# Gather, pair products and quad-diagonal moments of a recommendation tower: loops unrolled, weights laid out by the host, masks by VectorE, steps of eight groups, four row buffers

## The reference

```python
e = stack([tbl_f[ids[:, f]] for f in range(26)], axis=1)      # 512 x 26 x 32
def _cin_layer(x_prev, x0, W, b):
    return einsum('bik,bjk,hij->bhk', x_prev, x0, W) + b[None, :, None]
x1 = _cin_layer(e, e, W1, b1)                                  # W1: 128 x 26 x 26
x2 = _cin_layer(x1, e, W2, b2)                                 # W2: 128 x 128 x 26
z = sum(concatenate([x1, x2], axis=1), axis=-1)                # 512 x 256
h = concatenate([z, dense_ctx], axis=1)                        # 512 x 272
h = maximum(h @ W_top1 + b_top1, 0.0)                          # 512 columns
h = maximum(h @ W_top2 + b_top2, 0.0)                          # 256 columns
y = h @ W_top3                                                 # 512 x 1
```

## Time and profile before

| | |
|---|---|
| Median of three timed runs | 189.18 us (188.01 to 190.05) |
| Span of the profiled execution, first to last instruction | 269.0 us |
| The profiled execution's own time, with what lies around the span | not recorded for this run |
| PE / DVE / ACT / POOL busy | 171.1 / 94.1 / 103.7 / 109.4 us |
| Mean granted PE clock in the span | 0.797 of full speed |
| Instructions | 3544 |

### The profile page before, as it was taken

How to read it: one execution, slowest core, us unless ns; L and a number is a source line. 1 busy time by engine, 2 the same in 40 slices (tenths; PEclk the granted TensorE clock), 3 DMA queues, 4 the chain that set the end, 5 groups by cost and what they waited for, 6 DMA issues and landing times.

```text
span 269.0 us, 3544 instructions
## 1 busy us (share of the span) xinstructions
PE 171.1 (64%) x1239; PEld 158.7 (59%) x1239; DVE 94.1 (35%) x370; ACT 103.7 (39%) x267; POOL 109.4 (41%) x110
## 2 busy tenths in 40 slices
PE   7900594209929388986300799954001999899997
PEld 7800583209729287976300789954002999888985
DVE  0576003210943086920000568500003569047200
ACT  1020330019595165494000462951003463966313
POOL 3778777720077400577774003877770000000000
PEclk9975598556997869996555599995555799999999
DMA  6700011000001000011000000001000000000000
GB/s 240 250 12 13 12 14 14 13 7 0 0 10 17 11 1 4 2 12 15 14 12 10 0 0 2 11 12 15 12 12 2 0 0 0 0 0 0 0 0 3
DMA packets 5729, 5.08 MB, mean 19 GB/s; under 512 B 2875, under 2 KB 5061, under 8 KB 5718
## 3 DMA queue, kind: packets, MB, share of 16 engines
q0 software_dynamic: 3328, 1.71, 4.7%
q1 hardware_dynamic: 1698, 2.34, 2.6%
q10 hardware_dynamic: 692, 0.89, 1.0%
HBM read 4.93 MB, written 0.00 MB: 18 GB/s over the span
## 4 chain that ended last, share of the span: by engine, by line
PE 35%; another core or an unknown queue 30%; ACT 15%; DVE 9%; issue 9%; POOL 0%; DVEq 0%; ACTq 0%; POOLq 0%
PE bank L321 9%; ACT diag L467 8%; PE bank L287 4%; DVE t L650 4%; PE bank L322 4%; PE bank L281 4%; PE bank L256 3%; PE bank L332 2%; DVE prod L771 2%; PE bank L372 1%; ACT w2t L432 1%; ACT t L486 1%; DVE prod L616 1%; PE bank L275 1%
## 5 line engine op out<-in xcount | busy, mean ns | idle before, releaser
L242 POOL DMA_INDIRECT rows<-in_tbl_dram,idx x104 | 108.7, 1045 | 91.1 <-DVE prod L616 57.4
L321 PE MATMUL bank<-diag,prod 128*128 128x108 f32 x256 | 60.7, 336 | 56.0 <-DVE t L650 44.3
L321 PEld LDWEIGHTS bank<-diag,prod 128*128 128x128 f32 x256 | 46.6, 227 | 59.5 <-issue 59.5
L650 DVE COPY t<-bank 13x64 f32<-13x64 f32 (+2 forms) x128 | 26.7, 209 | 108.6 <-ACT t L487 66.7
L322 PE MATMUL bank<-diag,prod 128*77 128x64 f32 x256 | 41.7, 249 | 0.3 <-issue 0.3
L322 PEld LDWEIGHTS bank<-diag,prod 128*77 128x77 f32 x256 | 36.8, 173 | 0.5 <-issue 0.5
L485 ACT COPY t<-bank 55x128 f32<-55x128 f32 x32 | 8.3, 259 | 71.9 <-remote 47.8
L467 ACT COPY diag<-prod 32x416 f32<-32x416 f32 (+2 forms) x48 | 33.4, 696 | 1.0
L287 PE MATMUL bank<-w1ab,w2t 128*128 128x169 f32 x52 | 16.0, 489 | 14.6 <-ACT folded L434 9.7
L287 PEld LDWEIGHTS bank<-w1ab,w2t 128*128 128x128 f32 x52 | 12.8, 278 | 17.5 <-ACT folded L434 10.4
L281 PE MATMUL bank<-w1s,w2t 128*128 128x183 f32 x52 | 10.8, 377 | 16.4 <-ACT w2t L432 15.6
(11 more groups left out here) (79 smaller groups left out, 186.3 us busy)
## 6 DMA issues: line engine op xcount, KB each, us to landing
rows<-in_tbl_dram,idx POOLq DMA_INDIRECT x104
wt<-in_W_top_dram SPq DMA_DIRECT2D x2, 512.0 KB
w<-in_L_rec_W_dram ACTq DMA_DIRECT2D x1, 832.0 KB
w<-in_L_rec_W_dram SPq DMA_DIRECT2D x1, 832.0 KB
w<-in_L_rec_W_dram SPq DMA_DIRECT2D x1, 338.0 KB
idx<-in_ids_dram SPq DMA_DIRECT2D x4, 13.0 KB
vec<-in_L_rec_b_dram ACTq DMA_DIRECT2D x2, 0.5 KB
dctx<-in_dense_ctx_dram ACTq DMA_DIRECT2D x1, 32.0 KB
```

The lines of the kernel that those rows point to most:

```text
L242: pool.indirect_dma_start(rows[:, f, :], None, tables[f], bass.IndirectOffsetOnAxis(ap=idx[i][:, f:f + 1], axis=0)).then_inc(s_got[part], 16)
L321: nc.tensor.matmul(m0[:, g * P:g * P + JW * QUADS], prod[:, G, 0:P], mov, start=True, stop=True)
L650: ins = nc.vector.tensor_copy(t1[p0:p0 + HALF, GRAM + slot:GRAM + slot + nb, n].rearrange("p j (g r) -> p j g r", r=QUADS), m1[64:64 + HAL ...
```

## The change

What is added, moved and removed, engine by engine:

- Host: `layouts` hands over W2 already transposed, the two halves of the symmetrized W1 in the column order of the pairs (`w1p`) and in transposed form (`w1t`), the vectors as columns, the dense context transposed and the indices of all tiles side by side. PE's transposes of W2, W1, vectors and context and ACT's copies of them go, as do DVE's 30 small operations that symmetrized W1. One DVE addition over 521 columns takes their place, and one for `z1w` (five blocks of 128 columns).
- Gathers: four row buffers and all indices from the start. POOL waits for nothing but the indices; its loop is unrolled.
- Masks: ACT's twelve copies in a tile (`fill_diag`) go. DVE writes `diag` with one multiplication for each part (`fields_in`), of the fields (repeated four times) by a 0/1 mask `quad`. That is a DVE operation with two inputs in SBUF of 13, 10 and 3 fields x 4 columns x 32 groups: 1664, 1280 and 384 elements in a partition.
- Steps: four steps of eight groups, three PSUM banks for each. `products_b` still takes four groups, but all eight calls of a tile now run in one row ahead of the copies out. ACT copies out five times in a step, and DVE four times.
- PE increments: a matmul no longer carries a semaphore increment. Each is on a `drain` behind it: 35 in the setup, and in a tile four in the moments, one each for z2, z1, layer 2 and layer 3, and four in layer 1.
- Order: the whole setup now precedes tile 0's moments. In a tile z2 comes ahead of z1. Layer 2's two halves share one bank and one increment. All loops over tiles are unrolled.

```diff
-GSTEP = 4
+GSTEP = 8
 STEPS = GROUPS // GSTEP
+GBANK = 4
+NBANK = GBANK * QUADS
 NSTEP = GSTEP * QUADS
+GPROD = 4
+PRODS = GROUPS // GPROD
...
+SETUP = [("fold", j, 2) for j in range(0, FIELDS, 2)]
+SETUP += [("ctA", x, min(3, HALF - x)) for x in range(0, HALF, 3)]
+SETUP += [("ctB", x, min(3, HALF - x)) for x in range(0, HALF, 3)]
+SETUP += [("v0", j, min(4, FIELDS - j)) for j in range(HALF, FIELDS, 4)]
+SETUP += [("v1", x, min(4, J1 - 1 - x)) for x in range(0, J1 - 1, 4)]
+SETUP += [("v0", j, min(4, HALF - j)) for j in range(0, HALF, 4)]
+DONE = {kind: q + 1 for q, (kind, first, n) in enumerate(SETUP)}
+FOLD_A = 1 + SETUP.index(("fold", HALF - 1, 2))
...
+        w1p = sb("w1p", [P, 2, PAIRS + 2 * CROSS])
+        w1t = sb("w1t", [P, 2, 1 + GSLOTS, H])
+        w2t = sb("w2t", [P, FIELDS, H])
...
+        quad = sb("quad", [P, QUADS])
...
-        idx = [sb(f"idx{i}", [P, FIELDS], I32) for i in range(2)]
-        rows = sb("rows", [P, FIELDS, EMB])
+        idx = sb("idx", [P, TILES, FIELDS], I32)
+        rows = [sb(f"rows{t}", [P, FIELDS, EMB]) for t in range(TILES)]
...
+            sp.dma_start(idx[:, 0, :], io["ids"][:, 0, :]).then_inc(s_idx[0], 16)
+            sp.dma_start(w1p[:], io["w1p"]).then_inc(s_w1p, 16)
+            sp.dma_start(idx[:, 1:TILES, :], io["ids"][:, 1:TILES, :]).then_inc(s_idx[1], 16)
+            sp.dma_start(w2t[:, 0:HALF, :], io["w2t"][:, 0:HALF, :]).then_inc(s_w2, 16)
...
-            with nc.gpsimd.Fori(0, TILES // 2) as u:
-                for i in range(2):
-                    pool.wait_ge(s_idx[i], u * 16 + 16)
-                    for part, (f0, f1, _) in enumerate(PARTS):
-                        pool.wait_ge(s_turn[part], u * 2 + i + 1)
-                        pool.sem_inc(s_go, 1)
-                        for f in range(f0, f1):
-                            pool.indirect_dma_start(
-                                rows[:, f, :], None, tables[f],
-                                bass.IndirectOffsetOnAxis(ap=idx[i][:, f:f + 1], axis=0)).then_inc(s_got[part], 16)
+            for t in range(TILES):
+                if t < 2:
+                    pool.wait_ge(s_idx[t], 16)
+                for part, (f0, f1, _) in enumerate(PARTS):
+                    for f in range(f0, f1):
+                        pool.indirect_dma_start(
+                            rows[t][:, f, :], None, tables[f],
+                            bass.IndirectOffsetOnAxis(ap=idx[:, t, f:f + 1], axis=0)).then_inc(s_got[t][part], 16)
...
+                nc.tensor.drain().then_inc(s_su, 1)
...
+            def moments(t):
                 pe.wait_ge(s_pa, t + 1)
                 for s in range(STEPS):
-                    m0, m1 = MOM[s % 2]
-                    pe.wait_ge(s_pb, t * STEPS + s + 1)
-                    if s == 1:
-                        pe.wait_ge(s_h1, (t + 1) * MT1)
+                    b0 = 3 * (s % 2)
+                    if s == 1 and t:
+                        pe.wait_ge(s_h1, t * MT1)
                     if s >= 2:
                         pe.wait_ge(s_e0, t * STEPS + s - 1)
                         pe.wait_ge(s_eg, t * STEPS + s - 1)
                     for g in range(GSTEP):
                         G = s * GSTEP + g
+                        if G % GPROD == 0:
...
+                            pe.wait_ge(s_pb, t * PRODS + G // GPROD + 1)
...
+                    nc.tensor.drain().then_inc(s_mom, 1)
...
+                    nc.tensor.matmul(L1[m][:, 0:P], wt1[:, 0, chunk(m)], z[0][:], start=False, stop=True)
+                    nc.tensor.drain().then_inc(s_l1, 1)
...
+            for t in range(TILES):
                 moments(t)
-                mlp2(t - 1, L2)
-                z2_b(t)
-                z1(t)
-                mlp3(t - 1)
-                z2_second_chunk()
-                z2_a()
-                mlp1(t)
-            mlp2(TILES - 1, L2_LAST)
-            mlp3(TILES - 1)
+                if t:
+                    layer2(t - 1)
+                pe.wait_ge(s_e0, t * STEPS + STEPS)
+                z2_low()
+                if t:
+                    layer3(t - 1, L3)
+                z2_high()
+                pe.wait_ge(s_eg, t * STEPS + STEPS)
+                if t:
+                    pe.wait_ge(s_y, t)
+                else:
+                    pe.wait_ge(s_z1w, 1)
+                z1()
+                layer1(t)
+            layer2(TILES - 1)
+            layer3(TILES - 1, L3_LAST)
...
+            def evict(t):
                 for s in range(STEPS):
-                    m0, m1 = MOM[s % 2]
-                    n = slice(s * NSTEP, (s + 1) * NSTEP)
-                    act.wait_ge(s_mom, t * STEPS + STEPS + s + 1)
-                    if s == 0:
-                        act.wait_ge(s_z, t * 2 + 2)
-                    def view(m, p, js, width):
-                        return m[0:p, 0:GSTEP * width].rearrange("p (g j r) -> p j g r", g=GSTEP, r=QUADS)[:, js]
-                    def dst(x, p0, p, js):
-                        return x[p0:p0 + p, js, n].rearrange("p j (g r) -> p j g r", r=QUADS)
-                    w = J1 * QUADS
-                    nc.scalar.copy(dst(t1, 0, C1, slice(0, GRAM)), view(m1, C1, slice(0, J1, 2), w))
-                    nc.scalar.copy(dst(t1, 64, C1, slice(0, GRAM - 1)), view(m1, C1, slice(1, J1 - 1, 2), w))
-                    nc.scalar.copy(dst(t1, 0, C1, slice(GRAM, GRAM + 1)),
-                                   view(m1, C1, slice(J1 - 1, J1), w)).then_inc(s_e1, 1)
-                    nc.scalar.copy(dst(t0, 0, P, slice(0, JW)), view(m0, P, slice(0, JW), P)).then_inc(s_e0, 1)
-                    if s < len(between):
-                        take(between[s])
-            def copy_z1(t):
-                act.wait_ge(s_z, t * 2 + 3)
-                nc.scalar.copy(z[0][:], Z1[:, 0:P]).then_inc(s_zs, 1)
-            def copy_z2(t):
-                act.wait_ge(s_z, t * 2 + 4)
-                nc.scalar.activation(z[1][:], Z2[:, 0:P], ACT.Identity, bias=b2x32[:, 0:1]).then_inc(s_zs, 1)
+                    b0 = 3 * (s % 2)
+                    act.wait_ge(s_mom, t * STEPS + s + 1)
+                    if s == 0 and t:
+                        act.wait_ge(s_z1, t)
+                    n0 = s * NSTEP
+                    def low(p0, p, slots, js):
+                        src = bank[b0 + 2][0:p, :].rearrange("p (g j r) -> p j g r", g=GSTEP, r=QUADS)[:, js]
+                        dst = t1[p0:p0 + p, slots, n0:n0 + NSTEP].rearrange("p j (g r) -> p j g r", r=QUADS)
+                        return nc.scalar.copy(dst, src)
+                    low(0, C1, slice(0, GRAM), slice(0, J1, 2))
+                    low(64, C1, slice(0, GRAM - 1), slice(1, J1 - 1, 2))
+                    low(0, C1, slice(GRAM, GRAM + 1), slice(J1 - 1, J1))
+                    for b in range(GSTEP // GBANK):
+                        src = bank[b0 + b][:].rearrange("p (g j r) -> p j g r", g=GBANK, r=QUADS)[:, 0:JW]
+                        n = n0 + b * NBANK
+                        ins = nc.scalar.copy(t0[:, :, n:n + NBANK].rearrange("p j (g r) -> p j g r", r=QUADS), src)
+                    ins.then_inc(s_e0, 1)
...
+                n = f1 - f0
+                dve.wait_ge(s_got[t][part], 16 * n)
+                nc.vector.transpose(prod[:, :, col:col + n].rearrange("p g f -> p f g"),
+                                    rows[t][:, f0:f1, :]).then_inc(s_turn[part], 1)
+                dve.wait_ge(s_turn[part], t + 1)
+                nc.vector.tensor_tensor(diag[:, :, f0:f1, :],
+                                        with_dims(prod[:, 0, col:col + 1], (PCOLS, GROUPS), (1, n), (0, QUADS)),
+                                        with_dims(quad[:, 0:1], (0, GROUPS), (0, n), (1, QUADS)), ALU.mult)
...
+                for s in range(PRODS):
+                    products_b(nc.vector, prod, s * GPROD, GPROD).then_inc(s_pb, 1)
+            def bands(t):
+                if t:
+                    dve.wait_ge(s_z1, t)
+                for s in range(STEPS):
+                    m1 = bank[3 * (s % 2) + 2]
+                    dve.wait_ge(s_mom, t * STEPS + s + 1)
+                    n = slice(s * NSTEP, (s + 1) * NSTEP)
+                    for p0, b, nb, slot in BANDS:
+                        ins = nc.vector.tensor_copy(
+                            t1[p0:p0 + HALF, GRAM + slot:GRAM + slot + nb, n].rearrange("p j (g r) -> p j g r", r=QUADS),
+                            m1[64:64 + HALF, :].rearrange(
+                                "p (g j r) -> p j g r", g=GSTEP, r=QUADS)[:, HALF - JLOW + b:HALF - JLOW + b + nb])
+                    ins.then_inc(s_eg, 1)
...
+            half_a(0)
+            dve.wait_ge(s_sf, DONE["ctB"])
+            cross = cross_b(folded, ct[1])
+            add(cross, 0, False)
+            add(cross, 1, True)
             half_b(0)
-            cross = cross_b(folded, ct[1])
-            dve.wait_ge(s_sf, done["ctB"])
-            third = -(-len(cross) // 3)
```

(12 more changed lines are left out.)

478 lines of the change are left out of this document (174 added, 304 removed).

## The result

The changed kernel takes 200.75 us (median of 4, 199.96 to 201.84), the kernel before beside it 188.68 us (188.01 to 190.05): ratio 1.0685, 95% interval 1.0604 to 1.0767, 12.1 us slower. The profiled execution after took 201.84 us with a span of 200.1 us, so 1.7 us lie around the span. The span of 269.0 us that the prediction had to read the earlier trace rows isn't that of a 189 us run. On two of the four chips that the experiments ran on, the kernel before itself took 274.12 and 269.57 us in runs without a profile, and those chips are told of apart. Medians are of all executions of a kernel; the ratios leave out every execution more than 1.5% above the kernel's fastest.

What follows compares the result with a forecast made beforehand. The prediction took POOL's gather stream as the bound: 189.2 us before, plus 8.7 for mask products, 0.7 for `products_b` in one row and 0.6 for the tail gave 199.2, so 199 us, range 181 to 210.

Steps and rivals of the forecast that it cites:

- The gather stream is the bound: POOL's 104 gathers, without a gap, set the end; through tile 3 they last until 147.1 us in a timed run.
- The 80 us of unnamed waiting: Waits without a named releaser in the earlier profile, taken to belong to the profiled execution and not to timed runs.
- Four row buffers, 0: On POOL, four row buffers and early indices remove only gate time; the stream has no gap already, so 0 us.
- Mask products, 8.7 us: DVE's new two-input products under the stream, 14.3 us, hold POOL's gathers for 61% of that: 8.7 us, bounds 1.6 to 14.3.
- The stream's end, +8.7 + 0.7 = +9.4: Last gather ends later: 8.7 us for the mask products and 0.7 for the eight `products_b` in one row.
- Tail, +0.6: Behind the last gather: drains +2.3 us, moments in four steps -1.6, layer 2 +0.4, ahead of the moments about -0.5.
- PE's chain: The other bound: tile 3's moments at 140 to 150 us against 150.4 by the stream, 0 to 11 us to spare.
- What lies around the span: Time of a timed run outside its span: 189.2 us median less a reckoned span of 183.7, so 5.5 us.
- little lock cost: Rival: new DVE products pass between gathers as `products_b` did; 192.1 us, 189.8 with the drains free; chance 0.12.
- faster: Rival: timed runs still hold late PE increments or POOL's gate, which drains and open buffers remove; 179 to 182 us; chance 0.26.
- even: Rival: both bounds are close, the stream relieved by some idle time and burdened by the lock; 188 to 191 us; chance 0.07.
- The strict reading of the lock: All new two-input DVE time under the gather stream is lost, 21 us, giving 211 us; chance 0.08.

Runs made afterwards that it cites:

- b4: The kernel before with four row and index buffers, POOL's and DVE's loops unrolled, nothing else: 189.08 us, ratio 1.003 to the kernel before.
- a6: The changed kernel without drains, each mask product made by four DVE operations with one tensor input and a per-partition scalar: 200.89 us, ratio 1.066.
- a2: The changed kernel with every PE increment back on the last matmul or transpose, no drains: 198.71 us, ratio 1.054 to the kernel before.
- a4: The changed kernel with only tile 0 gathered and its rows used by all tiles, 78 of 104 gathers left out: 195.89 us.
- a3: The changed kernel with masks copied by ACT again and PE increments on matmuls, no drains: 191.48 us, ratio 1.017 to the kernel before.
- b1: The kernel before with masks by DVE's products instead of ACT's copies, on a slow chip: 263.19 us against 274.12, ratio 0.962.
- b5: The kernel before with masks by DVE's products instead of ACT's copies, on another slow chip: 257.68 us against 269.57, ratio 0.949.

## Why the prediction was right, and where it was not

The forecast of 199.0 us was met by 200.75, and its mechanism by one pair of kernels. Point by point:

- The gather stream is the bound: right, for both kernels, by the chain (59 and 61% POOL). The stream of before, reckoned to 147.1, ended at 148.8 in b4.
- The 80 us of unnamed waiting are no part of the 189 us runs: right. That they "belong to the profiled execution" is wrong as put: they belong to a kind of chip. Whole kernels run at 270 us there without a profiler (the kernel before with spans of 265.8 to 269.0 us on the last of them), and the trace of before has DVE's 1.4 us steps of those chips. On which chip it was taken isn't recorded.
- Four row buffers, 0: right (b4).
- Mask products, 8.7 us: 7.4 measured on POOL, 7.2 in time. The mechanism was right down to the 0.82 us; the 61% should have been 52%, 7.4 of the same 14.3 us. The rows behind the 61% were three whole runs that each held one gather from near its start; in the changed kernel gathers also slipped through between the mask and the products. The cause given, two inputs, fell as the only one with a6, though two inputs held more (6.6 against 4.9 us behind 65 us).
- The stream's end, +8.7 + 0.7 = +9.4: measured +9.4, but partly by luck. Masks 7.4 or so; 3.7 more of gathers held by other work or at other moments (POOL in b4 112.7, in a2 123.2 of which the masks are 7.4: 3.1 left, and 0.6 between a2 and after); and 1.7 back because the first gather starts earlier, which I had left out. The setup's cross terms now run on DVE as one block beside the products, with gathers of up to 4.53 us at 48 us: a moved part that I priced at 0.
- Tail, +0.6: this is the term that was mis-sized, +3.9 by the table (-1.0 + 2.0 + 2.9). Drains 0.28 us each instead of 0.165 (3.9 instead of 2.3, near my upper end of 4.2; from one execution of each kernel): the price of a filled pipeline was taken from the end of one matmul, while at a step's end the drain cost a whole group's time. Four steps instead of eight did take away b4's waits (three of 0.46 us), but six more half-speed groups cost 2.2 and turned that gain into a loss. Layer 2 with one increment, +0.4: 20.1 against 19.4 without drains, +0.7, with the new order of the layers in it. Ahead of the moments, -0.5: measured -1.0.
- PE's chain: too early. Tile 0's moments, reckoned to 48 us for the changed kernel, began at 61.6. Tile 3's, reckoned to 140 to 150 for the kernel before, began at 158.1 in the changed kernel without the stream (a4); for the kernel before no run shows them without it. In a2, without the setup's 35 drains, tile 0's moments began at 50.4; the granted clock of the folds was 0.83 there (12 to 31 us) and 0.68 in after (12 to 44 us). The cover that I gave as 0 to 11 us was about 3 in a4's profiled execution.
- What lies around the span: 1.7 us, not 5.5. Of the 3.8 us between, 0.7 is b4's shorter execution (188.53), 1.7 the stream's end (148.8, reckoned 147.1), 0.7 the way from there to the moments (4.0, reckoned 3.3) and 0.7 the tail (34.0, reckoned 33.3).

The rivals: "little lock cost" (189.8 to 192.1) fell with a2 less a3; "faster", which hoped for leftover stalls in the timed runs, fell with b4; "even" fell with the result. The strict reading of the lock in the Trainium skill, "SBUF — State Buffer", section "SBUF: two separate sides" (211), over-priced the products: by the timelines only DVE work that meets a gather and outlasts it costs. That the sum came so near is in part luck, since errors of both signs met: 1.3 us too much for the masks and 1.7 left out at the stream's start, against 3.0 too little for the other gathers and 3.3 too little for the tail. So the forecast 10.0 us became 13.3 in the profiled pair, and 12.1 by the medians.

## What to carry to other kernels

Where a stream of indirect DMAs issued by POOL sets the end, DVE's time is not free, however idle DVE looks: the mask products cost POOL about half their length here (7.4 of 14.3 us), so price such work there before moving work from ACT to DVE. Drains with the increments cost 2 us while the stream covered most of them, and 23 to 25 us, with the lower clock that came along, where PE's chain was the bound. Before reading stretches of nameless waiting as the kernel's, compare the span with the timed runs, and read a profile from an execution of the same length.

## What the hardware showed that I had not expected

- One-input DVE products hold a gather too (2.06 us instead of 0.95 at 142.13 us of a6), though less than two-input ones: 4.9 against 6.6 us over the gathers behind 65 us.
- Eight two-input products of 0.46 us in a row cost the gathers beside them 0.1 to 0.4 us each in after and a2, and held one for 3.96 us in a6.
- PE at full load ran at half speed for 6.1 us after a pause of only 2.1 us (0.51 from 161.2 to 167.3, having been at 1.00 until 159.1). In b4 it stood for 4.75 us and ran at half speed for 3.2.
- The same program takes 188 to 189 us on two chips and 270 to 274 us on two others, where PE issues one instruction every 1.4 us as long as POOL's gathers stream. Which change pays is different there: masks on DVE were a loss of 7 us on a quick chip (in the changed kernel, a2 against a3) and a gain of 4 to 5% on the slow ones (in the kernel before, b1 and b5).
